# State-space layer: delta and its product one state later; quantised layer: a pair finished behind the quantisation of two pairs on

## What is computed

```python
# quantised layer (blocks of 32 columns, a grid of 6-bit floats)
xq, xs = _mx_quantize(x2)
wq, ws = _mx_quantize(w2)
out = (xq * xs[..., None]).reshape(x2.shape) @ wd.T + bias

# state-space layer (256 channels, 16 states)
xn = _layernorm(x, ln_gamma, ln_beta)
u, res = jnp.split(xn @ W_in + b_in, 2, axis=-1)
u = jax.nn.silu(causal convolution of u over 4 rows + conv_b)
dt, Bm, Cm = jnp.split(u @ W_x, [64, 80], axis=-1)
delta = jax.nn.softplus(dt @ W_dt + b_dt)
# for each row t:  h = exp(delta_t * A) * h + (delta_t * u_t) * B_t ;  y_t = h . C_t
y = (y + u * D) * jax.nn.silu(res)
return y @ W_out + b_out + x
```

## Time and profile before

| | |
|---|---|
| median of three runs | 2640.59 us (2640.28 to 2643.39) |
| the profiled execution, its own time | 2641.36 us |
| its span, first to last instruction | 2639.6 us |
| mean granted TensorE clock | 0.864 of full speed |
| busy over the span: TensorE, VectorE, ScalarE, GpSimd | 2032.7, 1710.9, 1390.5, 1209.5 us |
| quantised layer | 811 to 905 us |
| state-space layer | 1717 to 2300 us |

### The profile page before, as it was taken

One profiled execution on the slowest core, in us unless ns is written; L12 is line 12 of the kernel. 1 busy time (PEld: TensorE's weight loads), 2 busy tenths in 40 slices (PEclk: granted clock), 3 DMA queues, 4 the chain that ended last, 5 costly groups with the idle time before them and its releaser, 6 DMA issues. The chain is left out here.

```text
span 2639.6 us, 49063 instructions
## 1 busy us (share of the span) xinstructions
PE 2032.7 (77%) x16544; PEld 1509.7 (57%) x16544; DVE 1710.9 (65%) x4178; ACT 1390.5 (53%) x2993; POOL 1209.5 (46%) x1233
## 2 busy tenths in 40 slices
PE   5999999999986783196599996858888888732870
PEld 3666666666775673175255555746677776531560
DVE  5777777777667573012677773759999999846113
ACT  4665656575432373032265554658888888520223
POOL 5655545464310005454321213557777777501662
PEclk8999999999996595598599997979999999955885
DMA  8300000000020000122333340000000000010113
GB/s 240 84 2 2 1 2 2 2 1 2 2 72 0 0 0 32 57 67 78 96 82 86 85 131 1 0 1 1 0 0 0 0 0 0 0 32 8 46 43 97
DMA packets 104254, 89.49 MB, mean 34 GB/s; under 512 B 12076, under 2 KB 91206, under 8 KB 104006
## 3 DMA queue, kind: packets, MB, share of 16 engines
q1 hardware_dynamic: 96934, 72.67, 10.2%
q0 software_dynamic: 7168, 14.73, 1.8%
HBM read 59.02 MB, written 40.96 MB: 38 GB/s over the span
## 5 line engine op out<-in xcount | busy, mean ns | idle before, releaser
L3342 POOL TENSOR_SCALAR mb_w<-mb_duT,mb_bT 128x256 f32<-128x256 f32 x384 | 354.8, 944 | 110.5 <-ACT mb_duT L3220 99.3
L3278 DVE TENSOR_TENSOR_SCAN mb_hs<-mb_dA,bank 128x512 f32<-128x512 f32 x256 | 302.2, 1206 | 16.7 <-PE bank L3377 10.1
L38 POOL TENSOR_TENSOR scrap<-ones 128x1 f32<-128x1 f32 x64 | 12.5, 195 | 470.1 <-DVE gla_ss L414 262.7
L3328 ACT ACTIVATE mb_dA<-mb_delta,mb_A 128x255 f32<-128x255 f32 x512 | 216.5, 496 | 0.2
L2083 ACT ACTIVATE e_hid<-bank,e_b 128x512 f32<-128x512 f32 (+1 forms) x128 | 79.3, 634 | 256.3 <-PE bank L2127 188.5
L3377 PE MATMUL bank<-ident,mb_w 128*128 128x128 f32 x1024 | 160.7, 287 | 65.4 <-DVE mb_hs L3278 56.3
L2501 DVE TENSOR_REDUCE ra_mx<-bank 128x2 f32<-128x512 f32 x256 | 163.7, 685 | 61.6 <-PE bank L2355 59.1
L2591 ACT ACTIVATE ra_pT<-bank 128x512 f32<-128x512 f32 x256 | 141.2, 600 | 114.5 <-PE bank L2377 114.2
L3377 PEld LDWEIGHTS bank<-ident,mb_w 128*128 128x128 f32 x1024 | 119.6, 148 | 96.2 <-DVE mb_hs L3278 68.7
L3399 PE MATMUL bank<-ident,mb_hc 128*128 128x128 f32 x1024 | 143.4, 285 | 31.7 <-DVE mb_hc L3288 31.4
L565 DVE TENSOR_TENSOR gla_mid<-bank,gla_ex 128x512 f32<-128x512 f32 x128 | 88.3, 690 | 122.5 <-ACT gla_ex L551 122.4
(11 more groups left out here) (541 smaller groups left out, 5784.7 us busy)
## 6 DMA issues: line engine op xcount, KB each, us to landing
results<-const_empty SPq DMA_DIRECT2D x2, 4096.0 KB
e_got<-results SPq DMA_DIRECT2D x32, 256.0 KB, 3.4
rope_rows<-ra_part SPq DMA_DIRECT2D x48, 128.0 KB, 1.9
ra_k<-rope_rows SPq DMA_DIRECT2D x32, 192.0 KB
ra_q<-rope_rows SPq DMA_DIRECT2D x32, 192.0 KB
queue<-const_spare_rows SPq DMA_DIRECT2D x1, 4128.0 KB
e_x<-queue SPq DMA_DIRECT2D x8, 516.0 KB
e_w<-in_L_ffn_w SPq DMA_DIRECT2D x2, 2048.0 KB, 8.2
```

What stands on the lines that cost most here:

```text
L3278: dve.tensor_tensor_scan(hs[n // 2 % 2][:, n % 2, :, :].rearrange("p c t -> p (c t)"), dA[n % RD][:, :, :].rearrange("p c t -> p (c t)"), ...
L3328: ins = act.activation(dA[n % RD][:, c, 1:SEQ], delta[k][:, c, 1:SEQ], ACT.Exp, scale=A[:, c, n:n + 1])
L3342: ins = pool.tensor_scalar(w[n % RH][:, h, :], duT[k][:, h, :], bT[k][:, h, n:n + 1], None, ALU.mult)
```

## The change

In the quantised layer VectorE quantises pairs 0 and 1 ahead of its loop, the loop quantises i+2 and finishes i, and pairs 6 and 7 are finished behind it. The second pair's quantisation, now outside the loop, keeps its wait for the transposes of the first. In the state-space layer delta and du (VectorE's stage 6) stand at n=11 instead of n=10, the transposes of du (TensorE's stage 6) at n=12 instead of n=11, and the copy duT (ScalarE's stage 8) at n=12 instead of n=11; stage 9 stays at n=11. At n=12 ScalarE's own work is the decay of state 0 of the next sequence (L3498), TensorE's is the inputs of state 14, a sum and a broadcast.

```diff
             def quantised(i):
                 for u in U:
-                    if not isinstance(i, int):
+                    if not isinstance(i, int) or i:
                         dve.wait_ge(xT_psum[u], i)
                     dve.wait_ge(xn_ready[u], i + 1)
...
             quantised(0)
-            with dve.Fori(0, NSEQ // 2 - 1) as i:
-                quantised(i + 1)
+            quantised(1)
+            with dve.Fori(0, NSEQ // 2 - 2) as i:
+                quantised(i + 2)
                 finished(i)
+            finished(NSEQ // 2 - 2)
             finished(NSEQ // 2 - 1)
...
-    DVE_WHEN = {6: (4,), 8: (5,), 9: (7,), 10: (6,)}
-    ACT_WHEN = {1: (0,), 3: (1, 2), 7: (4,), 8: (5,), 9: (6,), 11: (8, 9)}
-    PE_WHEN = {0: (0,), 1: (1,), 2: (2,), 6: (4,), 7: (5,), 8: (7,), 10: (9,), 11: (6,)}
+    DVE_WHEN = {6: (4,), 8: (5,), 9: (7,), 11: (6,)}
+    ACT_WHEN = {1: (0,), 3: (1, 2), 7: (4,), 8: (5,), 9: (6,), 11: (9,), 12: (8,)}
+    PE_WHEN = {0: (0,), 1: (1,), 2: (2,), 6: (4,), 7: (5,), 8: (7,), 10: (9,), 12: (6,)}
```

## The result

The changed kernel takes **2663.25 us** (median of 5 runs, 2655.55 to 2672.36), the kernel before 2641.49 us beside it (5 runs, 2640.28 to 2643.39): ratio 1.0079, 95% interval 1.0061 to 1.0097. It is slower, by 20.9 us by the ratio. The forecast was 2654.0, with a range to 2668.

The account below looks back on a forecast made before the run. The bound was taken as a loop through logarithm, ScalarE, TensorE's dense stretch, scan 5 and VectorE's full queue. 2641.36 + 13.0 (14 x 0.93), other terms 0, gave 2654.4, stated as 2654.0; range 2640 to 2668.

Parts of the forecast that it names:

- one mechanism: State-space layer: later duT delays GpSimd's w, then TensorE's sum, ScalarE's copy and the convolution; 14 x 0.93 = 13.0 us.
- the last step: Final sum: 2654.4, said to lie 0.8 us above the median of three runs, was stated as 2654.0.
- Delta and du: VectorE, state-space layer: delta's wait falls from 1.65 to 0.35 us; the 1.30 us are lost in waits for scans 0 to 5.
- duT and w: ScalarE and GpSimd: duT starts 5.96 us after delta instead of 3.73, GpSimd's w 6.65 instead of 4.42.
- The term per sequence, 0.93 us: TensorE's last sum starts at 2030.99 instead of 2030.06; this lateness makes the period 35.33 us, counted 14 times.
- The step that failed: Low clock falling on the sum or du also delays duT: taken as 0 extra, with an upper bound of 12.3 us.
- slower by more: Rival: a new gap before the first inputs lowers the clock over sum or dense stretch, up to 2666; no separate chance.
- my own case: State-space layer slower through late w, 2654.0 us, range 2646 to 2667, chance 0.76.
- The rule on gaps: TensorE: moving du's transposes could spare or spread the disturbed sequences' 0.70 us; sum about 12 us instead of 13.
- VectorE is the bound: Rival: the dense stretch only follows VectorE, so 14 sequences gain 1.30 us each, 18.2 us, to 2623; chance 0.12.
- Hidden: Rival: GpSimd starting at most 1.30 us later leaves the sum at 2030.06, about 2641 us; chance 0.12.
- Quantised layer, 0 between -0.5 and +1 us: Quantised layer: the loop of TensorE and ScalarE holds no finish; waits for x become waits for rows, no time change.

Follow-up runs that it names:

- the fourth experiment: Changed kernel plus 12 unread identity transposes on TensorE at n=12 and at n=14; 2650.06 us, ratio 1.0045 to the kernel before.
- the third experiment: Kernel before with delta and du moved to n=11 and duT to n=12, du transposes left at n=11; 2649.2 us, ratio 1.0042.

## Why the prediction was right, and where its sizes were off

The forecast was slower, by 13.0 us and through one mechanism. The ratio is 20.9 us slower, the time lies in the range, and the mechanism is the one named, with a second one on top that I had put at 0. By the fourth experiment the named one makes about 12 of the 20.9 us and the clock about 9: without the room left for the clock above 2654, the time would not have been inside. One slip is in the last step: 2654.4 less 0.8 is 2653.6, and not 2654.0.

- **Delta and du.** "Still waits 0.35 us for the logarithm": it waits 0.33 to 0.36. That the relief of VectorE is "lost in waits for scans 0 to 5" is seen in the scan waits, which grew by 31.7 us.
- **duT and w.** duT was put at 5.96 us after delta and starts at 5.87, since stage 9 starts 3.69 us after delta where I took 3.73, and the two pieces moved past take 1.38 and 0.80 us (1789.20 to 1790.58 to 1791.38) where I took 1.41 and 0.82. GpSimd was put at 6.65 and starts at 6.53. The sum follows at 12.57 where it was put 12.69 after delta. These are short by 0.12 us, and the chain of steps holds: moving duT alone gives 35.16.
- **The term per sequence, 0.93 us, was 0.74.** 0.12 us of the difference is GpSimd's earlier start. The other 0.07 us is between the sum and the convolution, 2.06 us apart before and 2.00 after. I had assumed that the lateness passes on in full. The eight transposes of the last sum take 1.04 us instead of 1.09, which is most of it. 14 x 0.74 = 10.4 us instead of 13.0.
- **The step that failed is the low clock's: "It is there in some sequences before and its cost is in the time before, so I take 0 for the difference."** Its cost rose from 1.0 to 8.8 us in the profiles, which is inside the bound of 12.3 that I had set beside it. In the kernel before, the du transposes follow at once on the inputs that end the gap. In four of the seven sequences with a low clock it falls only behind them, and only three of 14 periods are over 34.40 (34.49, 34.77 and the 35.10 of the earlier trace rows). After, eight transposes of the sum at n=12 stand in between as well; du's are slow in 7 of 14 sequences, and those periods are longer by 0.61 to 1.64 us. Both the "slower by more" rival and my own case were true in part. The cause that I named there was a new gap in front of the first inputs. That gap alone is cheap, as the third experiment shows. The dear one is the gap at n=12, ahead of the inputs of state 14, from which TensorE's move took the du transposes away.
- **The rule on gaps.** In the Trainium skill, TensorE: Matmul & The Clock Gate, section Why this matters for your kernels, long gaps between bursts bring the clock down. That filling TensorE's gaps keeps the clock at 2.4 GHz is what the fourth experiment shows (0.93 to 1.00). But that page of the Trainium skill speaks of gaps over about 3 us, and here the clock fell behind gaps of 2.43 us and less, in some sequences and not in others (see the last section). My use of the rule was wrong: I let it spare low stretches, where the change made more of them, and the sum by it, about 12 us, was further off than the one by the rows.
- **What bounds the kernel, and "VectorE is the bound."** The rival's price was wrong: moving delta alone gives 34.15 us and not 33.1. Its condition, that ScalarE's path and w must both be ahead, was right, and with both met the period is 33.37. But my own reading, that the loop runs through ScalarE's row with VectorE beside it, was wrong by a hair. Relieving ScalarE alone gave nothing (34.40), relieving VectorE alone gave 0.25 us. VectorE's path to the last sum was the bound, and ScalarE's row lay 0.22 us behind. I had taken a row without brackets for one without waits.
- **"Hidden".** Its point was a w up to 1.30 us late; it came 2.11 us late, and the margin that I called one overlooked slack was not there.
- **Quantised layer, 0 between -0.5 and +1 us.** 92.02 us and 92.04 us. Right, with the waits changing places as said.
- **Last sequence and what lies behind it, 0.** 379.3 and 379.2 us from the last delta to the end. Right, though this stretch scatters by more from kernel to kernel.

Open: why the first period differs by over 1 us (34.37 to 35.72), the first delta by up to 13 us and the end behind the last delta by up to 7 us (375.5 to 382.9) from kernel to kernel. No edit reaches what lies ahead of the first delta but the quantised layer's, which is as long in the three profiles in which I measured it. No run bears on these. That the spread of the runs (2655.55 to 2672.36 for the changed kernel) also comes from where the low stretches fall is argued, since each run but one has no profile.

## To carry to other kernels

An engine with the largest busy share and a regular wait can be the bound by very little: here the next path (ScalarE's copy) lay 0.22 us behind it, so 1.30 us of relief gave 0.25 us, and 1.03 us once that path had been cleared as well. Walk each chain once round the loop, and ask how far behind the second one is. On an engine that works in order, a step moved by one place costs what stands in that place, here 2.1 us for a copy, and the copy's reader on another engine pays it; so an early producer's start should stay where it is when only a neighbour's wait is to be removed. Of three moves made together, try each alone: here one gains 0.4%, one loses 0.4%, and one loses 2%.

## What the hardware did that I hadn't expected

- The granted clock can fall behind gaps of TensorE that are short. In the disturbed sequence shown above TensorE waits 1.98 us before the inputs at 1858.61, and the windows read 1.00 until 1860 and 0.63 from 1860 to 1862, then 0.50:

```profile
1858.00:1860.00 2.00, 0.93 (x6) 0.69 (x7) 2.00 (x4) 2.00 (x6) 0.00 (x0) 1.00 0.00 0
1860.00:1862.00 2.00, 2.00 (x14) 1.88 (x13) 2.00 (x3) 1.93 (x5) 0.00 (x0) 0.63 0.00 0
1862.00:1864.00 2.00, 1.10 (x6) 0.69 (x4) 1.91 (x2) 1.72 (x5) 1.03 (x2) 0.50 0.00 0
```

- The length of the longest gap doesn't decide it. A wait of TensorE of 2.43 us is in nearly every sequence of the kernel before and of the one with only duT moved; the clock falls in 7 of 14 sequences of the one and in 10 of the other. With waits of about 2.0 us and of 1.8 to 2.6 us (the changed kernel) it falls in 13 of 14. With delta and duT moved there are 0.86 and 0.47 us around the du transposes and then up to 2.92 us for w: 12 of 14, and in three of them it falls ahead of the wait for w. With delta alone moved no wait is above 1.18 us, and no sequence has it. But with the earlier copy added to that no wait is above 0.99 us, and three of 14 sequences have it, at no cost to the period:

```profile
2115.03 1.97 PE L3399 MATMUL bank<-ident,mb_hc 128*128 128x128 f32 x8 [0.46 <-DVE mb_hc L3288]
```

  Filling two gaps kept the clock up (fourth experiment). What makes it fall in one sequence and not in the next is open.
- The same low clock has quite different prices. It costs nothing in the kernel with only duT moved, where 10 of 14 sequences have it, up to 0.3 us a sequence with delta and duT moved, and 1.64 us in the worst sequences of the changed kernel. The mean granted clock doesn't tell its price; the durations on the path do.
- Sequences of equal work come out unequal, in an irregular pattern (35.14, 35.36, 36.78, 35.18, 35.85 us and so on in the changed kernel). I had read one sequence of each kind, and the rare kind became every second one.
